# Cross keys halved into differences on PSUM scores, with part of the row maxima formed by ScalarE and VectorE together, in a post-norm decoder layer

## The chip, the cores and the metric

The kernel runs on one core of a Trainium2 chip. The metric is the device time of one execution in microseconds (us): the median of several runs. One core has TensorE (PE in the profile; its weight loads, PEld, overlap the matmuls), VectorE (DVE), ScalarE (ACT), GpSimd (POOL) and SyncE (SP), which issues most transfers.

## The reference, cut to what matters

```python
x = layernorm(x + linear_attention(x))                 # 16 heads of 64, relu features
q, k, v = heads(x @ Wq + bq), heads(x @ Wk + bk), heads(x @ Wv + bv)     # 8 x 512 tokens, 16 heads of 16
y  = softmax(causal(q @ k.T * scale)) @ v              # 512 keys
qc, kc, vc = heads(x @ Wcq + bcq), heads(ctx @ Wck + bck), heads(ctx @ Wcv + bcv)
y += softmax(qc @ kc.T * scale) @ vc                   # 1024 context keys: the cross attention
x = layernorm(x + y @ Wp + bp)
x = layernorm(x + top1_of_8_experts(x))                # 256 -> 1024 -> 256
```

Batch 8, 512 tokens, width 256, context 1024 x 128, all float32. The softmax subtracts the maximum of each query's scores over all of its keys.

## The kernel before, in words

A loop over the 8 batches does both attentions, and the experts follow once at the end. Inside a batch the second attention, the stretch that the change is about, works on 8 pairs of heads. The two heads of a pair (`a` = 0 and 1) lie on partitions 0 to 63 and 64 to 127 of `hq` and `hk`, so two neighbouring matmuls of different heads run on the two halves of TensorE's rows at the same time. Every head needs its scores twice.

- **Maxima units** (`("max", p, m)`, 22 a pair): scores with queries on the partitions, 128 queries by 512 keys, one matmul into one PSUM bank (`max_unit`), then one VectorE pass (`reduce`) writes the maximum of each row to `craw`. Sixteen of them are cross units (4 query tiles, 2 halves of the 1024 keys, 2 heads), read by a plain `reduce_max`; six are self units, read by `tensor_tensor_reduce` with the causal mask added.
- **Row units** (`("row", p, 0)`): the finished maxima `mpad` are turned by TensorE, and four ScalarE copies write them to `mrow`.
- **Exp units** (`("exp", p, n)`, 11 a pair: 3 own, 8 cross): scores with keys on the partitions, both heads, 4 matmuls of 512 columns in a cross unit. Two of them are the scores; the other two (`minus`, `mrow`) subtract the maximum inside PSUM (L826). Then one ScalarE exponential of 128 x 1024 goes to the ring `es`. The units use two slots of two banks in turn, so unit k waits for the exponential of k-2.
- **Weigh units**: the exponentials times the values, 8 matmuls into a bank of their own, `zbank`. After the last of a pair, `keep` (ScalarE, `zk`) copies it out, `turn` (TensorE L867) transposes it into a ring bank and ScalarE writes `zt`.

Maxima, rows and turns share three PSUM banks as a ring: each takes the bank that has been free longest, and TensorE waits for the last reader of that bank (`ring_slot`). In the first stretch of a batch there is a fourth bank, `zbank`.

`heads_order` writes one list, ORDER, which every engine follows in the same order. First come 30 maxima units (22 + `AHEAD` of 8), with projections between them (`FIRST_PARTS`). Then comes a loop in which each turn, called a **cycle** in this document, has on TensorE: one maxima unit (A), exp unit k, two maxima units (B, C), exp unit k+1, one maxima unit (D), two weigh units of four units earlier. 11 cycles make two pairs, called a **period** here. The maxima run ahead of the exponentials, so the last cycles of a batch have none.

`kc0` and `kc1` are the cross key projections: ScalarE writes their high part to `stage` and VectorE the rest (`high_part`, `low_part`).

## Time and profile before

| | us |
|---|---|
| median of 3 runs | 2242.48 (2242.23 to 2243.74) |
| the profiled execution | 2242.68 |
| its span in the profile | 2240.8 |
| one batch (start to start) | 235 |
| of it: 30 maxima units with projections between | 22 |
| of it: 44 cycles | 128 |

The profiled execution stands 0.20 us above the median, and 1.9 us of it lie outside the span, so a change of the span is read as a change of the time. One batch out of the middle of the loop (its second attention at 572 to 723 us) is read closely; the others are alike.

### The profile page before, as it was taken

Reading aid. Unit: us, or ns where it says so; the run is one execution under the profiler, and the core shown is the slowest. Engines: PE = TensorE matmul, PEld = TensorE weight load, DVE = VectorE, ACT = ScalarE, POOL = GpSimd, SP = SyncE. Lnnn points to the kernel's source line nnn. Section 1 sums busy time; section 2 is a strip of 40 time slices with the busy share of each in tenths; the row PEclk is TensorE's granted clock in tenths of the full one; section 3 lists DMA queues with packets and bytes.
Section 4 is the critical chain, followed back from the end, with each engine's and each line's share of the span. In section 5 each row is a group of like instructions: output and inputs, shape, how many; then the busy total and the mean of one; then the engine's idle time right before and its main releaser. Section 6 shows DMA issues by size and latency. Waiting matters only on the chain. (4 is left out here: it accounts for less than half of the span.)

```text
span 2240.8 us, 51067 instructions
## 1 busy us (share of the span) xinstructions
PE 2155.1 (96%) x16290; PEld 1349.3 (60%) x16291; DVE 1364.8 (61%) x3905; ACT 1100.7 (49%) x1680; POOL 367.4 (16%) x628
## 2 busy tenths in 40 slices
PE   8999999999999999999999999999999999799998
PEld 4555555556455555555555555565556455599997
DVE  2588358844784468645883588358844785354454
ACT  1267525761477237722774267525762477233332
POOL 1011111111111111111111111111111111122222
PEclk9999999999999999999999999999999999899999
DMA  7440035102610162005400450035102610755553
GB/s 239 158 167 25 1 110 204 47 2 86 226 49 2 65 224 72 2 11 208 141 2 11 153 173 25 1 108 204 48 2 86 226 49 1 245 186 179 177 182 110
DMA packets 115762, 235.74 MB, mean 105 GB/s; under 512 B 19614, under 2 KB 42655, under 8 KB 113344
## 3 DMA queue, kind: packets, MB, share of 16 engines
q1 hardware_dynamic: 112112, 224.23, 29.9%
q0 software_dynamic: 3408, 8.41, 1.0%
q8 instruction: 136, 2.23, 0.4%
q14 instruction: 106, 0.87, 0.1%
HBM read 154.04 MB, written 73.17 MB: 101 GB/s over the span
## 5 line engine op out<-in xcount | busy, mean ns | idle before, releaser
L1221 ACT ACTIVATE es<-ps 128x1024 f32<-128x1024 f32 (+1 forms) x704 | 665.0, 984 | 241.4 <-PE ps L826 178.7
L1432 DVE TENSOR_REDUCE craw<-ps 128x1 f32<-128x512 f32 x1024 | 636.0, 683 | 95.7 <-PE ps L790 93.9
L790 PE MATMUL ps<-hk,hq 64*128 64x512 f32 x1024 | 382.6, 449 | 13.3 <-DVE craw L1428 5.6
L824 PE MATMUL ps<-hq,hk 64*128 64x512 f32 x1024 | 323.1, 436 | 2.2 <-ACT es L1221 2.2
L826 PE MATMUL ps<-mrow,minus 64*128 64x512 f32 x1024 | 285.6, 390 | 0.0
L1428 DVE CUSTOM_DVE_ANT_0 ps<-ps,causal 128x512 f32<-128x512 f32 (+3 forms) x512 | 235.7, 519 | 74.7 <-PE ps L787 74.3
L790 PEld LDWEIGHTS ps<-hk,hq 64*128 64x128 f32 x1024 | 173.8, 184 | 177.3 <-DVE craw L1432 119.1
L856 PE MATMUL ps<-es,vca 128*17 128x256 f32 x4096 | 276.7, 382 | 1.1
L678 POOL TENSOR_SCALAR_AFFINE_SELECT es<-es 128x256 f32<-128x256 f32 x256 | 99.0, 406 | 619.6 <-ACT es L1221 619.4
L1751 ACT ACTIVATE hT<-ph,b1s 128x128 f32<-128x128 f32 x312 | 89.0, 368 | 183.3 <-PE ph L1714 183.3
L826 PEld LDWEIGHTS ps<-mrow,minus 64*128 64x128 f32 x1024 | 165.4, 185 | 10.6
L824 PEld LDWEIGHTS ps<-hq,hk 64*128 64x128 f32 x1024 | 141.9, 184 | 29.6 <-ACT es L1221 18.6
L856 PEld LDWEIGHTS ps<-es,vca 128*17 128x17 f32 x4096 | 93.8, 96 | 107.7 <-issue 35.7
L1714 PEld LDWEIGHTS ph<-xinT,w1s 128*128 128x128 f32 x1248 | 147.5, 194 | 3.0 <-issue 1.1
L1714 PE MATMUL ph<-xinT,w1s 128*128 128x128 f32 x1248 | 147.8, 277 | 0.7 <-ACT xinT L1741 0.7
L1727 PE MATMUL py<-w2s,hT 128*128 x624 | 141.1, 379 | 0.0
L787 PE MATMUL ps<-hk,hq 64*128 64x512 f32 (+3 forms) x512 | 139.0, 349 | 0.5
L876 PE MATMUL ps<-xT_s,wqf 128*128 128x512 f32 x288 | 138.4, 607 | 0.0
L886 PE MATMUL ps<-wkf,xT_s 128*128 128x512 f32 x288 | 130.3, 597 | 0.0
L817 PE MATMUL ps<-hq,hk 64*128 64x512 f32 (+3 forms) x512 | 125.6, 340 | 0.6
L1727 PEld LDWEIGHTS py<-w2s,hT 128*128 128x128 f32 x624 | 115.5, 190 | 14.1
L787 PEld LDWEIGHTS ps<-hk,hq 64*128 64x128 f32 x512 | 81.0, 184 | 66.1 <-issue 25.4
(210 smaller groups left out, 2833.4 us busy)
## 6 DMA issues: line engine op xcount, KB each, us to landing
w1s<-in_w1T SPq DMA_DIRECT2D x39, 1024.0 KB, 5.4
hk<-scr_kc SPq DMA_DIRECT2D x64, 512.0 KB, 5.1
scr_kc<-staged SPq DMA_DIRECT2D x16, 1024.0 KB, 4.2
scr_qc<-staged SPq DMA_DIRECT2D x32, 512.0 KB, 4.5
scr_q<-staged SPq DMA_DIRECT2D x32, 512.0 KB, 5.3
hq<-scr_qc SPq DMA_DIRECT2D x56, 256.0 KB, 4.5
hq<-scr_q SPq DMA_DIRECT2D x56, 256.0 KB, 4.2
hk<-scr_k SPq DMA_DIRECT2D x56, 256.0 KB, 4.6
```

What stands on the lines that cost most here:

```text
L787: last = mm(pb[:, col:col + w], hq[i][at, t * P:(t + 1) * P], hk[i][at, 0:w], start=True, stop=True)
L790: last = mm(pb, hq[i][at, T + t * P:T + (t + 1) * P], hk[i][at, T + half * BANK:T + (half + 1) * BANK], start=True, stop=True)
L824: mm(pb[a], hk[i][rows[a], T + j * P:T + (j + 1) * P], hq[i][rows[a], T:2 * T], start=True, stop=False)
L826: last = mm(pb[a], neg[a], mrow[p % 2][rows[a], :], start=False, stop=True)
L856: last = mm(z[row:row + VW, (2 - len(tiles)) * P:2 * P], (va if own else vca)[:, j, p * HB + a, :], weights, start=n in (0, NSELF), stop=n ...
L876: last = mm(t[:, a * T:(a + 1) * T], wqf[:, c, j * P:(j + 1) * P], xT_s[:, c, :], start=c == 0, stop=c == KC - 1)
L886: last = mm(t[:, half * 512:(half + 1) * 512], xT_s[:, c, i * P:(i + 1) * P], wkf[:, c, half * 512:(half + 1) * 512], start=c == 0, stop=c ...
L1221: nc.scalar.activation(es[:, k % ERING, :].rearrange("p (a c) -> p a c", a=HB)[:, :, 0:w], eslot[k % 2][:].rearrange("p (a c) -> p a c", a ...
L1428: last = v.tensor_tensor_reduce(own, own, causal[:, (NT - 1 - t) * P:NT * P], 1.0, LOWEST, ALU.add, ALU.max, craw[p % 2][:, t, a:a + 1, 0])
L1432: last = v.reduce_max(craw[p % 2][:, t, a:a + 1, 1 + half], pb, AX.X)
L1714: last = mm(ph[g % 2][:, a * TILE:(a + 1) * TILE], w1s[i][:, k, (GROUP * c + a) * P:(GROUP * c + a + 1) * P], xinT[i][:, k, :], start=k == ...
L1727: last = mm(py[i][:, n, 0:C], hT[i][:, c, n * P:(n + 1) * P], w2s[:, bass.ds(e * (NHC * C) + c * C, C)], start=c == 0, stop=c == NHC - 1)
```

## The change

The first half of the cross keys is stored as a difference: GpSimd subtracts the two halves of the context once a batch (`context_difference`), so that `kc` columns 0 to 511 hold key j minus key j+512, without bias, and columns 512 to 1023 hold the second half itself. Scores of the first half are then scores of the second half plus scores of the difference, and they are formed by adding a matmul onto the bank that still holds the former.

- Exp units: a cross tile of the second half is done as before. The tile of the first half ("rest") is two units later in the same slot and has two matmuls of differences only; the maximum is still subtracted there. Own and cross units are reordered so that each rest unit follows its tile by two.
- Maxima units: the rest unit of a query tile must use the same bank as its first unit. Therefore the ring is replaced by fixed places: head 0 always uses bank 1 (banks 1 and 3 in turn for the first pair), and head 1, rows and turns use banks 0 and 2 in turn.
- For head 1 and the last two query tiles the two halves are not added in PSUM. Unit "over" gets the differences and ScalarE writes their positive part to `over_s` (`maxima_over`); unit "upper" gets the second half, and VectorE adds `over_s` and takes the maximum in one pass. VectorE has 20 passes a pair in place of 22, ScalarE two more.
- `AHEAD` is 12 in place of 8 and `ROW_AFTER` (8, 6) in place of (4, 6); a cycle is now A, exp, B, exp, C, D, weigh, weigh.

```diff
-AHEAD = 8
-ROW_AFTER = (4, 6)
+AHEAD = 12
+ROW_AFTER = (8, 6)
...
+def cross_tile(c):
+    i = c // 4 * 2 + c % 2
+    return (i, True) if c % 4 >= 2 else (NTC // 2 + i, False)
+OWN_UNITS = [("own", i, False) for i in range(NSELF)]
+CROSS_UNITS = [("cross", *cross_tile(c)) for c in range(NTC)]
+UNITS = (OWN_UNITS + CROSS_UNITS, OWN_UNITS[:2] + CROSS_UNITS + OWN_UNITS[2:])
...
+BY_TILE = [("cross", t, rest) for t in range(NT) for rest in (False, True)]
+BY_TWO = [("cross", 2 * n + t, rest) for n in range(NT // 2) for rest in (False, True) for t in range(2)]
+SHARED = BY_TWO[:NT] + [("over" if over else "upper", t, False) for t in range(NT // 2, NT) for over in (True, False)]
+def max_of(p, m):
+    n, a = divmod(m, HB)
+    cross = SHARED if a else BY_TWO if p == 0 else BY_TILE
+    return (*(cross + SELF_MAX if p % 2 or p == 0 else SELF_MAX + cross)[n], a)
...
 def heads_order():
-        order += take(HB)
+        order += take(1)
         if k + 1 < steps:
             order.append(("exp", *divmod(k + 1, NU)))
-        order += take(1, True)
+        order += take(HB, True)
...
 def places():
-        at = min(banks, key=lambda i: last[i])
+        if kind == "max" and m % HB == 0:
+            at = (1, 3)[count[0] % 2] if p == 0 else 1
+            count[0] += 1
+        else:
+            at = (0, 2)[count[1] % 2]
+            count[1] += 1
...
 def exp_scores(b, p, n):
-                        mm(pb[a], hk[i][rows[a], T + j * P:T + (j + 1) * P], hq[i][rows[a], T:2 * T], start=True, stop=False)
-                    for a in turned:
-                        last = mm(pb[a], neg[a], mrow[p % 2][rows[a], :], start=False, stop=True)
+                        last = mm(pb[a], hk[i][rows[a], T + j * P:T + (j + 1) * P], hq[i][rows[a], T:2 * T],
+                                  start=not rest, stop=rest, skip_group_check=rest)
+                    if not rest:
+                        for a in turned:
+                            last = mm(pb[a], neg[a], mrow[p % 2][rows[a], :], start=False, stop=True)
...
+                def maxima_over(p, m):
+                    e, t = ("max", p, m), max_of(p, m)[1]
+                    act.wait_ge(s_ring, cur(b, NRING, RING_AT[e] + 1))
+                    if p:
+                        act.wait_ge(s_red, cur(b, NRED, RED_AT[UPPER[p - 1, t]]))
+                    nc.scalar.activation(over_s[:, t - NT // 2, :], mbank[PLACE[e]], ACT.Relu).then_inc(s_over, 1)
...
+                    elif what == "upper":
+                        dve.sem_inc(s_held, 1)
+                        dve.wait_ge(s_over, cur(b, NOVER, OVER_AT["max", p, m]))
+                        dve.sem_inc(s_held, 1)
+                        last = v.tensor_tensor_reduce(pb, pb, over_s[:, t - NT // 2, :], 1.0, LOWEST, ALU.add, ALU.max,
+                                                      craw[p % 2][:, t, a:a + 1, 1])
```

What this does to TensorE's order at the start of a batch is seen after the second half of projection `qf0` (the first row, L930 or L876, is the projection). A row is one matmul with the PSUM tensor written, its inputs and the semaphores that it waits for; ps0 holds banks 0 and 1, ps1 bank 2 and `zbank`, and `s_red` is raised when VectorE has read a bank. Before:

```order
L876 MATMUL ps3<-xT_s,wqf 128x512 x2
L767 REGISTER_ALU
L790 MATMUL ps0<-hk1,hq1 128x512 [waits s_red]
L767 REGISTER_ALU
L790 MATMUL ps0<-hk1,hq1 128x512 [waits s_red]
L767 REGISTER_ALU
L797 ISA [waits s_red]
L798 MATMUL ps1<-ident,mpad 128x128 [waits s_max]
L767 REGISTER_ALU
L790 MATMUL ps1<-hk1,hq1 128x512 [waits s_red]
L739 REGISTER_ALU
L876 MATMUL ps2<-xT_s,wqf 128x512 [waits s_act]
```

After:

```order
L930 MATMUL ps3<-xT_s,wqf 128x512 x2
L819 REGISTER_ALU
L842 MATMUL ps0<-hk1,hq1 128x512 [waits s_red]
L819 REGISTER_ALU
L842 MATMUL ps0<-hk1,hq1 128x512 [waits s_red]
L819 REGISTER_ALU
L842 MATMUL ps0<-hk1,hq1 128x512 [waits s_red]
L819 REGISTER_ALU
L842 MATMUL ps1<-hk1,hq1 128x512 [waits s_red]
L789 REGISTER_ALU
L930 MATMUL ps2<-xT_s,wqf 128x512 [waits s_act]
L930 MATMUL ps2<-xT_s,wqf 128x512
```

Before, three maxima units and the row unit stood here in four different banks. Now there are four units, and the first and the third (both of head 0) are in bank 1.

In the cycle in which an even pair's result is turned (here pair 2, units 3 and 4 of pair 3 exponentiated), TensorE's rows from exp unit k+1 on were, before (`es,va` are weigh units, `zk` the turn):

```order
L824 MATMUL ps2<-hq1,hk1 128x512 [waits s_exp]
L824 MATMUL ps2<-hq1,hk1 128x512
L826 MATMUL ps2<-mrow1,minus 128x512 x2
L767 REGISTER_ALU
L787 MATMUL ps0<-hk2,hq2 128x512 [waits s_red]
L840 REGISTER_ALU [waits s_keep]
L856 MATMUL ps1<-es,va 17x256 [waits s_cut]
L856 MATMUL ps1<-es,va 17x256 x3
L767 REGISTER_ALU
L867 MATMUL ps1<-ident,zk 128x128 [waits s_keep,s_red]
L867 MATMUL ps1<-ident,zk 128x128 x3
```

The same cycle after the change:

```order
L875 MATMUL ps2<-hq1,hk1 128x512 [waits s_exp]
L875 MATMUL ps2<-hq1,hk1 128x512
L819 REGISTER_ALU
L842 MATMUL ps0<-hk2,hq2 128x512 [waits s_red]
L819 REGISTER_ALU
L842 MATMUL ps0<-hk2,hq2 128x512 [waits s_red]
L894 REGISTER_ALU [waits s_keep]
L910 MATMUL ps1<-es,va 17x256 [waits s_cut]
L910 MATMUL ps1<-es,va 17x256 x3
L817 REGISTER_ALU
L921 MATMUL ps1<-ident,zk 128x128 [waits s_keep,s_over]
L921 MATMUL ps1<-ident,zk 128x128 x3
```

The two `mrow` matmuls are gone, and the turn no longer waits for a pass of VectorE but for `s_over`: its bank was last used by the over unit of this same cycle, which ScalarE reads.

ScalarE's rows around it, after the change (`s_ring` is raised by a maxima unit, `s_sc` by an exp unit):

```order
L1288 ACTIVATE es<-ps3 128x1024 [waits s_av,s_sc]
L1278 REGISTER_ALU
L1280 REGISTER_ALU [waits s_ring]
L1281 ACTIVATE r_s<-ps1 128x512 [waits s_red]
L1286 REGISTER_ALU
L1288 ACTIVATE es<-ps2 128x1024 [waits s_av,s_sc]
L1297 ACTIVATE zk<-ps1 128x512 [waits s_av]
L1286 REGISTER_ALU
L1288 ACTIVATE es<-ps3 128x1024 [waits s_av,s_sc]
L1278 REGISTER_ALU
L1280 REGISTER_ALU [waits s_ring]
L1281 ACTIVATE r_s<-ps1 128x512 [waits s_red]
```

The rows on `r_s` are the new positive parts (`over_s` lies in `r_s`). The second one is what the turn waits for, and ahead of it stand an exponential, `zk`, another exponential and the positive part of the cycle before.

## Rows read from the trace of the kernel before

**Rows 1.** The page: busy time of each engine, share of the span, instructions.

```profile
PE 2155.1 (96%) x16290; PEld 1349.3 (60%) x16291; DVE 1364.8 (61%) x3905; ACT 1100.7 (49%) x1680; POOL 367.4 (16%) x628
```

**Rows 2.** Busy time by stretch: first maxima, one period, last cycles of a batch.

```profile
core 0: us, PE busy (x) PEld busy (x) DVE busy (x) ACT busy (x) POOL busy (x), PEclk, DMA share, GB/s
565.00:594.50 29.50, 28.57 (x90) 13.10 (x89) 21.04 (x44) 8.94 (x15) 4.22 (x4) 1.00 0.77 264
657.00:690.20 33.20, 32.50 (x342) 19.38 (x338) 27.74 (x68) 24.54 (x36) 5.26 (x12) 1.00 0.01 2
702.10:722.80 20.70, 19.46 (x227) 9.53 (x223) 2.20 (x12) 17.11 (x23) 3.35 (x8) 1.00 0.01 2
```

**Rows 3.** Timeline of TensorE, one cycle: units A and D, weigh, next A.

```profile
626.61 0.49 PE L790 MATMUL ps<-hk,hq 64*128 64x512 f32 x1
...
627.93 0.46 PE L790 MATMUL ps<-hk,hq 64*128 64x512 f32 x1
...
628.32 1.06 PE L856 MATMUL ps<-es,vca 128*17 128x256 f32 x16
629.30 0.49 PE L790 MATMUL ps<-hk,hq 64*128 64x512 f32 x1
```

**Rows 4.** Timeline of VectorE over the same cycle.

```profile
627.14 2.48 DVE L1432 TENSOR_REDUCE craw<-ps 128x1 f32<-128x512 f32 x4 [0.21 <-PE ps L790]
```

**Rows 5.** Groups by line and shape: count, busy, mean ns, idle before.

```profile
L1432 DVE TENSOR_REDUCE craw<-ps 128x1 f32<-128x512 f32 x1024 | 636.0, 683 | 95.7 <-PE ps L790 93.9
L826 PE MATMUL ps<-mrow,minus 64*128 64x512 f32 x1024 | 285.6, 390 | 0.0
L790 PEld LDWEIGHTS ps<-hk,hq 64*128 64x128 f32 x1024 | 173.8, 184 | 177.3 <-DVE craw L1432 119.1 <-DVE craw L1428 27.3 <-ACT mrow L1213 12.7
L1428 DVE CUSTOM_DVE_ANT_0 ps<-ps,causal 128x512 f32<-128x512 f32 x128 | 86.0, 713 | 40.8 <-PE ps L787 40.8
```

**Rows 6.** Timeline of TensorE, first maxima of a batch up to cycle 1.

```profile
588.86 0.51 PE L790 MATMUL ps<-hk,hq 64*128 64x512 f32 x2
...
589.98 1.98 PE L876 MATMUL ps<-xT_s,wqf 128*128 128x512 f32 x4
...
592.56 1.98 PE L876 MATMUL ps<-xT_s,wqf 128*128 128x512 f32 x4
594.47 0.49 PE L790 MATMUL ps<-hk,hq 64*128 64x512 f32 x1
```

**Rows 7.** Timeline of TensorE, the cycle with a turn: 646.96 to 650.92.

```profile
644.70 0.49 PE L790 MATMUL ps<-hk,hq 64*128 64x512 f32 x1
...
646.96 0.49 PE L790 MATMUL ps<-hk,hq 64*128 64x512 f32 x1
...
649.34 0.66 PE L867 MATMUL ps<-ident,zk 128*128 128x128 f32 x4
649.92 1.06 PE L856 MATMUL ps<-es,va 128*17 128x128 f32 x20
650.92 0.44 PE L787 MATMUL ps<-hk,hq 64*128 64x384 f32 x1
```

**Rows 8.** Timeline of ScalarE in that cycle and the one before.

```profile
645.75 1.51 ACT L1221 ACTIVATE es<-ps 128x1024 f32<-128x1024 f32 x2 [0.91 <-PE ps L820]
647.15 0.61 ACT L1230 ACTIVATE zk<-ps 128x512 f32<-128x512 f32 x1
```

**Rows 9.** Timeline of TensorE, a cycle with a row unit.

```profile
655.78 0.32 PE L798 MATMUL ps<-ident,mpad 128*128 128x128 f32 x1 [0.18 <-DVE craw L1432]
656.04 1.06 PE L856 MATMUL ps<-es,vca 128*17 128x256 f32 x16
```

**Rows 10.** Timeline of both engines in a last cycle: two exp units, weigh, next.

```profile
717.86 0.50 PE L824 MATMUL ps<-hq,hk 64*128 64x512 f32 x2
...
717.98 1.94 ACT L1221 ACTIVATE es<-ps 128x1024 f32<-128x1024 f32 x2 [0.17 <-PE ps L826]
...
719.50 0.51 PE L824 MATMUL ps<-hq,hk 64*128 64x512 f32 x2
```

More of the change, by code:

```diff
@@ L133, in take @@
         taken = []
-        while maxima and (count or maxima[0][0] == "row") and (border or maxima[0] != ("row", PAIRS - 1, 0)):
+        while maxima and (count or border and maxima[0][0] == "row"):
             count -= maxima[0][0] == "max"
@@ L172, with is_over @@
 ORDER = heads_order()
+def is_over(entry):
+    return entry[0] == "max" and max_of(*entry[1:])[0] == "over"
 def reciprocals_later():
@@ L188 @@
 RING_AT = {e: n for n, e in enumerate(RING)}
-N_FIRST = sum(e[0] in ("max", "row") for e in ORDER[:ORDER.index(("exp", 0, 0))])
 def places():
-    place, former, last = {}, {}, [-1] * (MBANKS + 1)
-    for n, e in enumerate(RING):
-        banks = range(MBANKS + (n < N_FIRST))
-        at = min(banks, key=lambda i: last[i])
-        place[e], former[e], last[at] = at, RING[last[at]] if last[at] >= 0 else None, n
+    place, former, last, count = {}, {}, {}, [0, 0]
+    for e in RING:
+        kind, p, m = e
+        if kind == "max" and m % HB == 0:
[4 more added lines that the diff above has]
+            count[1] += 1
+        place[e], former[e], last[at] = at, last.get(at), e
+        if kind == "max" and max_of(p, m)[2]:
+            what, t, _, a = max_of(p, m)
+            assert former[e][0] == "max" and max_of(*former[e][1:]) == (what, t, False, a) and former[e][1] == p
     return place, former
 PLACE, SAME = places()
-NRING, NRED = len(RING), sum(e[0] == "max" for e in RING) + 1
+NRING, NOVER = len(RING), sum(is_over(e) for e in RING)
+NRED = sum(e[0] == "max" for e in RING) - NOVER + 1
 LAST_TURN = ("turn", PAIRS - 1, 0)
-RED_AT = {e: sum(f[0] == "max" or f == LAST_TURN for f in RING[:n + 1]) for n, e in enumerate(RING)}
+RED_AT = {e: sum(f[0] == "max" and not is_over(f) or f == LAST_TURN for f in RING[:n + 1]) for n, e in enumerate(RING)}
+OVER_AT = {e: sum(is_over(f) for f in RING[:n + 1]) for n, e in enumerate(RING)}
+UPPER = {(p, max_of(p, m)[1]): ("max", p, m) for p in range(PAIRS) for m in range(MAXES) if max_of(p, m)[0] == "upper"}
 NEXP = PAIRS * NU
-LAST_IN_Z = max(RED_AT[e] for e in RING if PLACE[e] == MBANKS)
+LAST_IN_Z = max(RED_AT[e] for e in RING if PLACE[e] == 3)
 TILE = 128
@@ L694, in _ @@
                 for kind, p, n in ORDER:
-                    if kind == "exp" and n < NSELF:
-                        cut(p, n)
+                    if kind == "exp" and UNITS[p % 2][n][0] == "own":
+                        cut(p, n, UNITS[p % 2][n][1])
                     elif kind == "turn" and p < PAIRS - 1:
@@ L770, in max_unit @@
             def max_unit(b, p, m):
-                n, a = divmod(m, HB)
+                what, t, rest, a = max_of(p, m)
                 i = p % SLOTS
-                if (n, a) == (0, 0):
+                if (what, t, rest, a) == ("cross", 0, False, 0):
                     if p == 0:
@@ L777, in max_unit @@
                     pe.wait_ge(s_cross[i], b * CROSS[i] + CROSS_AT[p])
-                if (n, a) == (2 * NT, 0):
+                if (what, t, a) == ("self", 0, 0):
                     if p == 0:
@@ L783, in max_unit @@
                 pb, at = ring_slot(b, ("max", p, m)), slice(a * HROW, (a + 1) * HROW)
-                if n >= 2 * NT:
-                    for t, col in MAX_SELF[n - 2 * NT]:
-                        w = (t + 1) * P
-                        last = mm(pb[:, col:col + w], hq[i][at, t * P:(t + 1) * P], hk[i][at, 0:w], start=True, stop=True)
-                else:
-                    t, half = divmod(n, 2)
-                    last = mm(pb, hq[i][at, T + t * P:T + (t + 1) * P],
-                              hk[i][at, T + half * BANK:T + (half + 1) * BANK], start=True, stop=True)
+                if what == "self":
+                    for u, col in MAX_SELF[t]:
+                        w = (u + 1) * P
+                        last = mm(pb[:, col:col + w], hq[i][at, u * P:(u + 1) * P], hk[i][at, 0:w], start=True, stop=True)
+                else:
+                    keys = hk[i][at, T:T + BANK] if rest or what == "over" else hk[i][at, T + BANK:T + TC_]
+                    last = mm(pb, hq[i][at, T + t * P:T + (t + 1) * P], keys, start=not rest, stop=True, skip_group_check=rest)
                 last.then_inc(s_ring, 1)
@@ L809, in exp_scores @@
                 rows = [slice(a * HROW, (a + 1) * HROW) for a in range(HB)]
-                w = int(n >= NSELF)
+                what, j, rest = UNITS[p % 2][n]
+                w = int(what == "cross")
                 neg = [minus[at, w:w + 1].broadcast_to([HROW, P]) for at in rows]
-                turned = range(HB - 1, -1, -1)
-                if n < NSELF:
-                    for j, col in EXP_SELF[n]:
+                turned = (0, 1) if k % 2 else (1, 0)
+                if what == "own":
+                    for j, col in EXP_SELF[j]:
                         w = T - j * P
@@ L843, in weigh @@
                 z = zbank[:, 0:T // 2] if own else zbank[:, T // 2:T]
[L844 removed]
+                for j, col in (EXP_SELF[i] if own else [(i, 0)]):
                     first = j if own else 0
@@ L1288, in _ @@
             v.memset(blank, 0.0)
+            for n in range(2):
+                v.memset(craw[n][:], LOWEST)
             v.memset(mpad[:], 0.0)
@@ L1462, in _ @@
                 for kind, p, n in DVE_ORDER:
-                    if kind == "max":
+                    if kind == "max" and not is_over((kind, p, n)):
                         reduce(p, n)
```

70 lines of the change are left out of this document (46 added, 24 removed).

## Prediction

> **What bounds the kernel now.** I read the page first: TensorE is busy for 96% of the span, VectorE for 61%, ScalarE for 49% [rows 1]. By that alone TensorE is the bound and every matmul taken away is time won. Then I read the stretches of one batch, since the share is a mean. In one period of the maxima and exponentials (33.2 us) TensorE has 32.5 us busy, VectorE 27.7, ScalarE 24.5, but TensorE's weight loads only 19.4 [rows 2]. A matmul here has a mean of 390 ns [rows 5], although two of them on different row halves start every 0.23 us or so; its busy time holds pipeline depth and waiting. So I went to the timeline.
>
> In a regular cycle unit A starts at 626.61, D at 627.93, the weigh units at 628.32 and the next A at 629.30 [rows 3]. That is 1.32 + 0.39 + 0.98 = 2.69 us. VectorE starts on A at 627.14, 0.53 us after the matmul, and does four passes in 2.48 us, 0.62 each; before them it sat idle 0.21 us waiting for TensorE [rows 4]. A pass has a mean of 683 ns [rows 5], so A's pass ends at 627.82, and D, the fourth unit on a ring of three banks and thus in A's bank, starts 0.11 us later. The 1.32 us are therefore a round trip: matmul, 0.53 us, pass, release of the bank (0.79 us after the pass began). The work between A and D fits inside it. The 119.1 us that weight loads of L790 wait for VectorE [rows 5] are such places. A cycle is a latency chain A, pass, D, weigh, A, and neither engine's sum.
>
> The reader is to see that taking matmuls out of the stretch from A to D saves nothing as long as the round trip stays.
>
> **The Trainium skill on this reading.** "Trainium Kernel Development and Optimization", section Performance Expectations, says that matmul busy time is a bad measure of how near TensorE is to its limit, and that weight load time is a better one. By the former the removed matmuls would be worth their columns (the first rival below), by the latter TensorE has room. This trace agrees with the page: 32.5 of 33.2 us against 19.4 [rows 2].
>
> **The change, part by part.**
>
> *Matmuls removed.* Half of the 1024 `mrow` matmuls of the cross units [rows 5] go: 512, side by side in pairs, 256 slots of about 0.23 us, 59 us in all. In regular cycles they lie between A and D, under the round trip: 0.
>
> *Fixed places.* Head 0 is always in bank 1. The cycle is now A, exp, B, exp, C, D, and C must wait for A's bank. That is the same round trip, 1.32 us, now ahead of C. D (head 1) comes behind it with a weight load of its own; a load takes 184 ns [rows 5] and overlaps the former in part, so I take 0.1, bounds 0 and 0.18. A regular cycle: 1.32 + 0.1 + 0.39 + 0.98 = 2.79 us, against 2.69. The four cycles of a period without a keep, turn or self unit pay this, as do others.
>
> *VectorE passes.* Two per pair less (1.24 us). VectorE already waits in each cycle [rows 4], so 0 on the chain. The new pass with a second operand is not in the trace; the nearest is the masked one, 713 ns for 512 columns against 683 [rows 5]. With a float32 operand from SBUF I take the same; even 0.3 us more would fall into VectorE's 5.5 us of idle time per period [rows 2]. 0, bound +0.3 per pair.
>
> *ScalarE's positive part.* 128 x 512, not in the trace: nearest are the narrower exponential (1.51 less 0.92, thus 0.59 us) and `zk` (0.61) [rows 8]; starts follow each other after about 0.5 us. ScalarE has 8.7 us idle per period [rows 2] and two pairs cost 2.0, so mostly hidden. What is queued behind it is the next exponential and everything after. This hurts in one place, the turn of an even pair, whose bank was just used by an over unit. Before: the turn at 649.34, 4.64 us after the start (644.70) of the cycle before it; then 0.58 us to the weigh units and 1.00 to the next cycle [rows 7]. Now, from the same start: first exponential at 1.05 [rows 7, 8], positive part at 1.97, exponential at 2.46 (now 1024 wide in place of the narrow one), `zk` at 3.38, exponential at 3.87, positive part 4.79 to 5.38, the turn at about 5.45. The two cycles take 7.03 us, not 6.22: +0.8. Without this wait it would be +0.1 to +0.2. Behind the waiting turn stand all weigh units and the next maxima, so nothing covers it.
>
> *The other special cycles*, worked out the same way (release 0.79 after the start of a pass, self passes by the 713 ns row). A row unit waits for the second pass, 0.53 + 0.62 + 0.79 = 1.94, then 0.26 and 0.99: 3.19 us as now [rows 9]. The self units of an odd and an even pair now follow each other in bank 1, and cost about +0.2 in the odd turn's cycle (a round trip begun later, as VectorE still holds an upper unit), -0.2, +0.5 and -0.4 in the next three; a keep cycle with the narrow own unit gains 0.25. The sum over the eleven cycles is 33.8 us against 33.2 now [rows 2], and 33.1 in the period before it: +0.7, bounds -0.5 (no 0.1 for D and no wait at the turn) and +1.6 (0.18 for D, 0.3 per new pass).
>
> *The first maxima of a batch.* Here bank 1's round trip has no exp units above it. Before: 588.86 to 594.47, 5.61 us, with two projection halves of 1.91 [rows 6] between. After, from the same point: a group with two head-0 units, 1.32 + 0.1 + 0.33; a half, 1.91; a group in which moreover an over unit waits for the second pass, 1.94 + 0.31; a half, 1.92; and, as `AHEAD` is 12, a third group with the round trip of 1.32 before cycle 1. Together 9.15: +3.5 us. Bounds +2 (banks freed by 0.3 earlier in each of three groups, and VectorE, with two passes less to do, brings 0.5 into it) and +4. The earlier groups use four banks as before and stay.
>
> *The last cycles.* The maxima end one cycle earlier. That cycle was 3.4 us and becomes 2.1: -1.3. In the seven others each rest unit is 0.23 us shorter, but ScalarE's two exponentials take 1.94 us, the second exp unit waits for one (717.86), and its own chain to the next cycle is 1.64 [rows 10]. ScalarE is busy 17.1 of 20.7 us there [rows 2]. I take 0.1 a cycle, -0.6 (bounds 0 and -1.6). Sum -1.9, bounds -1.3 and -2.9.
>
> *Keys and context.* GpSimd is busy 16% of the span [rows 1] and subtracts for the next batch at the end of this one: 0. `kc1` is two ScalarE instructions and not one, ahead of VectorE's copy of `x1T`: +0.1 a batch, bounds 0 and 0.2.
>
> **Sum for a batch.** First maxima +3.5; cycles 1 to 3, 0; cycles 4 to 10, which are a period's last seven, +0.8; two periods +1.4; last cycles -1.9; keys +0.1. Together +3.9, times 8 is +31 us. Against the profiled execution of 2242.7, which is 0.2 above the median, this gives 2274 us. With the bounds, taken not all at one end, +1.2 to +6.5 a batch: 2252 to 2295.
>
> **Rivals.** *TensorE's columns count.* If D waits less than I think and cycles shrink with what they hold, 59 us go, and the first maxima still cost 3.5 x 8 = 28: 2242.7 - 59 + 28 = 2212; with those hidden too 2184, with half the gain 2241. For it: 32.5 of 33.2 us busy [rows 2]. Against it: A to D equals the round trip to 0.11 us [rows 3, 4]. It decides if C or D starts under 1.2 us after A. *VectorE's relief counts.* 27.7 us of 33.2 is the highest share after TensorE's [rows 2]; with 1.24 us less a pair a period would be up to 2.5 shorter, 2242.7 - 8 x 3 x 2.5 + 28 = 2211. Against it: its 0.21 us of idle time in every cycle. The two together: chance 0.18. "Perfetto Trace Analysis", section Optimizing Scalar/DVE Operations, advises giving work of a saturated DVE to ScalarE; by it the second rival would hold. The trace does not bear it out here, as VectorE waits in every cycle. *The banks cost less:* the turn does not wait and D comes at once; then +1.5 a batch, 2255, slower still: 0.12. *No change,* the first maxima costing 2 and the cycles gaining 0.3 each period: 2242 to 2246, 0.08.
>
> **Chances.** My forecast 0.62, the others as above. A measurement of this kernel tells about 0.2% (4.5 us) from no change. Faster 0.19, same 0.07, slower 0.74. The range that leaves out no more than 2 in 10 reaches from 2230 (part of the first rivals) to 2294; the likeliest case's own range is 2252 to 2295.
>
> **What would show it.** In the profile after: regular cycles of about 2.8 us with C 1.3 us after A and TensorE idle before it; the even turn at about 5.4 us from the start of the cycle before, released by ScalarE's `r_s`; the stretch from 588.86's counterpart to the first exp unit 9 us; weight loads of maxima units waiting for VectorE clearly above today's 119 us; busy VectorE about 80 us lower without a shorter span. Wrong would be cycles of 2.5 us or less, or a turn that is not held.

## The result and the profile after

| | before | after |
|---|---|---|
| median (us) | 2243.11 (2242.23 to 2243.82) | 2302.38 (2301.38 to 2304.52) |
| ratio | | 1.0265, 95% interval 1.025 to 1.0279 |
| profiled span | 2240.8 | 2299.7 |

The kernel is 59 us slower. The direction was forecast, the size (+31) was half of it, and the time lies above the range. First the page after, for [rows 1]:

```profile
PE 2139.2 (93%) x15778; PEld 1288.1 (56%) x15779; DVE 1334.8 (58%) x3907; ACT 1155.4 (50%) x1824; POOL 381.4 (17%) x637
```

TensorE and VectorE have less to do in a longer span. The groups after, with the columns of [rows 5]:

```profile
L1512 DVE TENSOR_REDUCE craw<-ps 128x1 f32<-128x512 f32 x768 | 501.5, 685 | 196.6 <-PE ps L842 192.4
...
L842 PEld LDWEIGHTS ps<-hk,hq 64*128 64x128 f32 x1024 | 143.7, 184 | 243.7 <-DVE craw L1512 196.4 <-issue 35.3 <-DVE craw L1503 10.3
...
L879 PE MATMUL ps<-mrow,minus 64*128 64x512 f32 x512 | 121.6, 392 | 0.0
...
L1509 DVE CUSTOM_DVE_ANT_0 ps<-ps,r_s 128x512 f32<-128x512 f32 x128 | 89.5, 699 | 23.2 <-ACT r_s L1281 23.2
```

Weight loads of maxima units wait 196 us for VectorE (119 before) while VectorE waits 192 us for those matmuls (94 before): each waits for the other. The new pass (L1509) has a mean of 699 ns, near the masked one's 713 [rows 5]. VectorE's busy time fell by 30 us and not by the 80 that the prediction names as a sign: 256 plain passes are gone (636.0 to 501.5 us), but 128 new ones came (89.5 us). The windows after: one period and the last cycles, for [rows 2]:

```profile
core 0: us, PE busy (x) PEld busy (x) DVE busy (x) ACT busy (x) POOL busy (x), PEclk, DMA share, GB/s
...
676.95:711.47 34.52, 32.11 (x327) 17.34 (x324) 26.95 (x69) 26.16 (x38) 5.36 (x13) 1.00 0.01 2
725.20:746.10 20.90, 19.48 (x224) 8.83 (x225) 0.95 (x5) 18.19 (x25) 3.75 (x8) 1.00 0.01 2
```

The period grew from 33.2 to 34.52 us at a full clock, with less busy time on TensorE. TensorE's timeline at the end of the first maxima, for [rows 6] (605.32 answers to 588.86, 614.52 to 594.47):

```profile
602.90 0.57 PE L842 MATMUL ps<-hk,hq 64*128 64x512 f32 x2 [1.09 <-DVE craw L1503]
603.40 1.98 PE L930 MATMUL ps<-xT_s,wqf 128*128 128x512 f32 x4
605.32 0.50 PE L842 MATMUL ps<-hk,hq 64*128 64x512 f32 x2
606.60 0.57 PE L842 MATMUL ps<-hk,hq 64*128 64x512 f32 x2 [0.78 <-DVE craw L1512]
607.10 1.98 PE L930 MATMUL ps<-xT_s,wqf 128*128 128x512 f32 x4
...
610.30 1.09 PE L842 MATMUL ps<-hk,hq 64*128 64x512 f32 x2 [0.52 <-DVE craw L1512]
...
614.52 0.49 PE L842 MATMUL ps<-hk,hq 64*128 64x512 f32 x1 [0.78 <-DVE craw L1512]
```

In every group the third unit, of head 0, waits for the pass on the first. The first row is one group earlier; its third unit waits 1.09 us for a self pass. TensorE's timeline of the cycle before the even turn and of the turn's, for [rows 7]:

```profile
666.94 0.50 PE L842 MATMUL ps<-hk,hq 64*128 64x512 f32 x1
...
668.32 0.48 PE L842 MATMUL ps<-hk,hq 64*128 64x512 f32 x2
668.73 0.63 PE L910 MATMUL ps<-es,vca 128*17 128x256 f32 x8
669.50 0.49 PE L842 MATMUL ps<-hk,hq 64*128 64x512 f32 x1
...
672.38 0.66 PE L921 MATMUL ps<-ident,zk 128*128 128x128 f32 x4 [0.19 <-ACT r_s L1281]
...
674.17 0.50 PE L842 MATMUL ps<-hk,hq 64*128 64x512 f32 x1
```

and VectorE's and ScalarE's beside it:

```profile
668.76 0.69 DVE L1512 TENSOR_REDUCE craw<-ps 128x1 f32<-128x512 f32 x1 [0.58 <-PE ps L842]
...
670.78 1.05 ACT L1288 ACTIVATE es<-ps 128x1024 f32<-128x1024 f32 x1
671.69 0.64 ACT L1281 ACTIVATE r_s<-ps 128x512 f32<-128x512 f32 x1
```

A starts at 666.94 and C, in the same bank, at 668.32: that is the round trip I had counted. But C's pass starts at 668.76 and the next A, again in bank 1, at 669.50: a second round trip in the same cycle, 1.18 us, which I had not. The turn starts 5.44 us after 666.94 (forecast 5.45), released by the positive part that stands behind exponentials. Since ScalarE holds the turn, the second round trip cost nothing in these two cycles; where nothing else holds TensorE, it does (see the cycles below). The two cycles take 7.23 us, not 7.03: behind the turn 1.20 us pass to the next A (672.97 to 674.17), 1.00 before [rows 7]. Here the Trainium skill ("Perfetto Trace Analysis", Optimizing Tensor Performance) bears: independent matmul groups should rotate through different PSUM banks, so that emptying one overlaps the next. The trace agrees: units that come back to a bank after two places wait, 0.78 us in the rows above.

Stretches of one batch, in us, read from the timelines of each kernel (start to start; zk is the copy of a pair's result, 0 to 7):

| kernel | first maxima to first exp | to zk 1 | zk 3 to 5, a period | zk 5 to 7 |
|---|---|---|---|---|
| before | 22.46 | 34.97 | 33.21 | 27.13 |
| after | 26.60 | 36.91 | 34.52 | 25.41 |
| e8_places | 26.70 | 35.31 | 33.60 | 26.38 |
| e2_over_first | 26.58 | 36.35 | 33.93 | 25.18 |
| e1_pad | 26.62 | 36.89 | 34.52 | 26.44 |
| e5_two_banks | 25.01 | 36.87 | 34.54 | 25.39 |
| e6_exp_only | 23.63 | 36.29 | 34.60 | 26.88 |
| e15_ring_fit | 26.31 | 36.30 | 34.01 | 26.57 |
| e17_ring_mixed | 22.36 | 35.83 | 33.63 | 26.79 |
| e19_ring_mixed_pad | 22.40 | 36.02 | 34.07 | 27.88 |

The period by its cycles, in us from A to A in the same batch. The eleven cycles are lettered as in the expectations below, and these letters are not those of the units: cycle C holds the odd turn and cycle I the even one, and in before cycles F and K hold row units. The cycle of [rows 3] is a B; 666.94 is the start of an H.

| cycle | before | e8_places | e2_over_first | after | e17_ring_mixed |
|---|---|---|---|---|---|
| C, odd turn | 3.67 | 3.94 | 3.94 | 4.04 | 3.95 |
| D | 2.71 | 2.64 | 2.86 | 2.86 | 2.49 |
| E | 3.02 | 3.19 | 3.70 | 3.70 | 2.69 |
| F | 3.19 | 2.70 | 2.70 | 2.69 | 3.10 |
| H | 2.26 | 2.78 | 2.56 | 2.57 | 2.49 |
| I, even turn | 3.98 | 4.15 | 4.13 | 4.66 | 4.28 |
| A, B, G, J, K | 14.35 | 14.22 | 14.00 | 14.00 | 14.61 |
| sum | 33.18 | 33.62 | 33.89 | 34.52 | 33.61 |

### The profile page after: what moved, and what is told of

Its sections match the earlier page's. It is cut to its first block and busy times, and to the rows that moved or that the text cites. A ratio compares the mean times of both kernels' runs of the same rounds, so it can differ in the third digit from the quotient of the medians.

```text
span 2299.7 us, 50687 instructions
## 1 busy us (share of the span) xinstructions
PE 2139.2 (93%) x15778; PEld 1288.1 (56%) x15779; DVE 1334.8 (58%) x3907; ACT 1155.4 (50%) x1824; POOL 381.4 (17%) x637
## 5 line engine op out<-in xcount | busy, mean ns | idle before, releaser
L1512 DVE TENSOR_REDUCE craw<-ps 128x1 f32<-128x512 f32 x768 | 501.5, 685 | 196.6 <-PE ps L842 192.4
L842 PE MATMUL ps<-hk,hq 64*128 64x512 f32 x1024 | 332.6, 467 | 52.1 <-DVE craw L1512 25.2
L910 PE MATMUL ps<-es,vca 128*17 128x256 f32 x4096 | 295.4, 383 | 0.0
L842 PEld LDWEIGHTS ps<-hk,hq 64*128 64x128 f32 x1024 | 143.7, 184 | 243.7 <-DVE craw L1512 196.4
L875 PE MATMUL ps<-hq,hk 64*128 64x512 f32 x1024 | 270.8, 444 | 7.5 <-ACT es L1288 4.4
L875 PEld LDWEIGHTS ps<-hq,hk 64*128 64x128 f32 x1024 | 124.8, 185 | 62.6 <-ACT es L1288 52.6
L839 PE MATMUL ps<-hk,hq 64*128 64x512 f32 (+3 forms) x512 | 119.2, 362 | 21.4 <-DVE craw L1503 15.4
L930 PE MATMUL ps<-xT_s,wqf 128*128 128x512 f32 x288 | 138.4, 607 | 0.0
L879 PE MATMUL ps<-mrow,minus 64*128 64x512 f32 x512 | 121.6, 392 | 0.0
L964 PE MATMUL ps<-big_b,x_s 128*128 128x512 f32 x256 | 119.9, 606 | 1.8 <-ACT big_b L1201 1.1
L839 PEld LDWEIGHTS ps<-hk,hq 64*128 64x128 f32 x512 | 67.5, 184 | 89.9 <-DVE craw L1503 71.2
L1061 PE MATMUL ps<-big_c,big_a 128*128 128x256 f32 x512 | 112.6, 381 | 2.9 <-ACT big_c L1241 2.9
```

Of the source, the lines that this page charges most:

```text
L839: last = mm(pb[:, col:col + w], hq[i][at, u * P:(u + 1) * P], hk[i][at, 0:w], start=True, stop=True)
L842: last = mm(pb, hq[i][at, T + t * P:T + (t + 1) * P], keys, start=not rest, stop=True, skip_group_check=rest)
L875: last = mm(pb[a], hk[i][rows[a], T + j * P:T + (j + 1) * P], hq[i][rows[a], T:2 * T], start=not rest, stop=rest, skip_group_check=rest)
L879: last = mm(pb[a], neg[a], mrow[p % 2][rows[a], :], start=False, stop=True)
L910: last = mm(z[row:row + VW, (2 - len(tiles)) * P:2 * P], (va if own else vca)[:, j, p * HB + a, :], weights, start=n == 0, stop=True, skip ...
L930: last = mm(t[:, a * T:(a + 1) * T], wqf[:, c, j * P:(j + 1) * P], xT_s[:, c, :], start=c == 0, stop=c == KC - 1)
```

## Experiments

Before ran beside every group of kernels, with medians of 2243.15 to 2243.62 us.

**e8_places: order and places alone.** The kernel before, with the order in a cycle, `AHEAD`, `ROW_AFTER` and `places()` of after; none of the new arithmetic, and own and self units where they were before.

```diff
-        order += take(HB)
+        order += take(1)
...
-        at = min(banks, key=lambda i: last[i])
+        if kind == "max" and m % HB == 0:
+            at = (1, 3)[count[0] % 2] if p == 0 else 1
```

> The kernel before (every unit with all its matmuls, no positive part on ScalarE, all 22 passes on VectorE), with only the order and the places of the kernel after: 34 maxima units ahead, A, exp, B, exp, C, D, head 0 always in bank 1. Theory (bank 1's two round trips in a cycle, C behind A and the next A behind C, cost the time): nearly all of the loss is here, 2280 to 2305 us, with a period of 34 us or more. Rival (the new work does it: the positive part on ScalarE, the pass with a second operand, the waits for ScalarE at the turns): 2243 to 2260 us.

Measured 2280.2 (ratio 1.0164, 1.0147 to 1.0181): +37 us. So most of the loss, not nearly all of it, is the schedule, and its period is 33.6 us, not the 34 or more that I expected. The table says where: +4.2 of its +4.6 us a batch are the first maxima, and a period has only +0.4. The order in a cycle and the places changed together here; no run parts them.

**e2_over_first: positive parts earlier.** On after:

```diff
+        if is_over(e) and order[n - 1][0] == "exp":
+            order[n - 1], order[n] = e, order[n - 1]
```

> The kernel after, ScalarE taking each positive part ahead of the exponential that it stood behind. Theory (the turn of the even pairs waits for the positive part behind two exponentials): the turn starts some 0.8 us earlier, three or four times a batch, 2277 to 2290 us. Rival (the wait at the turn is covered, or the exponential that is now later costs as much): 2297 to 2307 us.

Measured 2286.77: 15.6 us less than after. TensorE's timeline, cycle start and turn:

```profile
662.20 0.50 PE L854 MATMUL ps<-hk,hq 64*128 64x512 f32 x1
...
667.10 0.66 PE L933 MATMUL ps<-ident,zk 128*128 128x128 f32 x4
```

The turn now comes 4.90 us after that start, without a wait. The mechanism holds, 0.54 us at an even turn and 0.10 at an odd one (cycle C above).

**e1_pad: the removed columns put back.** On after, in a rest unit:

```diff
+                    if rest:
+                        for a in turned:
+                            last = mm(pb[a], nought[rows[a], 0:1].broadcast_to([HROW, P]), mrow[p % 2][rows[a], :], ...
```

> The kernel after, with two matmuls of zero weights added to each rest unit of the exponentials, so that all removed columns are back. Theory (a cycle is a chain of round trips): they fall into TensorE's waiting, +0 to +12 us on the kernel after (2302 to 2314), most of it in the last cycles of a batch. Rival (the columns count): 256 slots of 0.23 us, +59 us, 2361.

Measured 2307.8: +5.4 us. The page's groups show that both sorts of matmul are there, at one price:

```profile
L880 PE MATMUL ps<-mrow,nought 64*128 64x512 f32 x512 | 122.5, 391 | 0.0
L884 PE MATMUL ps<-mrow,minus 64*128 64x512 f32 x512 | 121.2, 390 | 0.0
```

The new group is 122.5 us of matmuls, TensorE's busy time rises by 34.5 us (2139.2 to 2173.7, as the matmuls overlap others), and the period stays at 34.52 us. Only zk 5 to 7 grows. The columns did not count, and this rival falls for the kernel as it is. The median hides a little of their price: undisturbed batches start 243.49 us apart, not 242.46, which is 8.2 us in all, but after lost some 2 us in two batches to what e1_pad's trace does not show (1.2 of it to the granted clock, see the last section).

**e5_two_banks: more banks for the first maxima.** On after:

```diff
-            at = (1, 3)[count[0] % 2] if p == 0 else 1
+            at = (1, 3)[count[0] % 2] if p == 0 or p == 1 and m < 8 else 1
```

So that the places fit, these units also take the query tiles in the order of pair 0.

> The kernel after, in which the first eight maxima units of pair 1 (still ahead of the exponentials) have banks 1 and 3 in turn for head 0 and not bank 1 alone. Theory (each unit that waits for its neighbour but one in bank 1 costs 0.5 to 0.8 us there, as nothing else lies between): 1.5 to 2.5 us less a batch, 2282 to 2291 us. Rival (the projections that stand between set the pace of that stretch): 2298 to 2306 us.

Measured 2290.56: 11.8 us less, 1.59 us a batch in the first column of the table and nothing elsewhere. Of the groups above, the one with 1.09 us of waiting has 0.27 left and the one with 0.78 none; the last two keep 0.38 and 0.78.

**e22_over_and_banks: both.**

> e2_over_first and e5_two_banks together on the kernel after. Theory (two separate waits at different places of a batch): their gains of 15.6 and 11.8 us add up, 2273 to 2278 us. Rival (they overlap): 2279 to 2288 us.

Measured 2273.52 (1.0135, 1.012 to 1.0151): 28.9 us less than after, where the two gave 27.4. They are separate terms.

**e6_exp_only: differences on the old ring.** The kernel before, rest units with two matmuls, and for half of the maxima units two matmuls added in a bank, followed by the same pass:

```diff
+                    last = mm(pb, hq[i][at, T + t * P:T + (t + 1) * P], hk[i][at, T + BANK:T + TC_], start=True, stop=half == 1)
+                    if half == 0:
+                        last = mm(pb, hq[i][at, T + t * P:T + (t + 1) * P], hk[i][at, T:T + BANK], start=False, stop=True)
```

> The kernel before with its ring of three banks and its order; keys as differences, rest units of the exponentials with two matmuls in place of four; the maxima of the lower half of the keys by two matmuls added in PSUM, with the same passes on VectorE. Theory (matmuls removed in the cycles bring nothing, only the last cycles of a batch gain, and the extra maxima matmuls lie under the round trip at a small cost): 2233 to 2250 us. Rival (the columns count): 512 matmuls come out in 256 slots of 0.23 us, and 512 go in, in part beside others: up to -59 and +0 to +59 us, and the period's length moves with what it holds, by over 0.5 us.

Measured 2284.96: +42 us, far outside what I expected, and the period is 34.60. TensorE's and VectorE's timelines of cycle B (L806 and L809 are the first and the added matmul):

```profile
674.34 0.50 PE L806 MATMUL ps<-hk,hq 64*128 64x512 f32 x1
674.68 0.39 PE L809 MATMUL ps<-hk,hq 64*128 64x512 f32 x1
...
675.90 0.45 PE L806 MATMUL ps<-hk,hq 64*128 64x512 f32 x1
677.27 0.49 PE L806 MATMUL ps<-hk,hq 64*128 64x512 f32 x1
```

```profile
675.11 2.49 DVE L1460 TENSOR_REDUCE craw<-ps 128x1 f32<-128x512 f32 x4 [0.44 <-PE ps L809]
```

VectorE starts 0.77 us after A and not 0.53 [rows 3, 4], D 1.56 us after it, and the cycle takes 2.93 us, not 2.69. I had put the added matmul under the round trip, but it stands in it. Six of the eleven cycles grow by 0.23 or 0.24 us like this one and cycle A by 0.17; cycles D, F and J do not change and cycle I loses 0.15. So here a removed matmul beside the chain gives nothing in most cycles, and an added one ahead of the pass costs all of its 0.24 us where the chain runs through it.

**e9_d_later.** The kernel before, D moved behind the weigh units:

```diff
-        order += take(1)
+        order += take(2 if k else 1)
...
-        order += take(1, True)
```

> The kernel before, with unit D of each cycle moved behind the two weigh units, next to A of the following cycle. Theory (a cycle of before is held by the round trip from A to D in one bank; the work between is shorter by some 0.1 us, and VectorE idles 0.21 us a cycle): cycles of 2.5 to 2.6 us in place of 2.69, 2205 to 2235 us. Rival (TensorE's own work fills the cycle, the round trip is covered): 2239 to 2247 us.

Measured 2365.79 (1.0551): +122 us, my worst miss but one. TensorE's and VectorE's timelines:

```profile
698.11 0.50 PE L789 MATMUL ps<-hk,hq 64*128 64x512 f32 x2
...
698.91 0.97 PE L789 MATMUL ps<-hk,hq 64*128 64x512 f32 x2
699.47 0.59 PE L816 MATMUL ps<-hq,hk 64*128 64x384 f32 x2
...
700.33 1.06 PE L855 MATMUL ps<-es,vca 128*17 128x256 f32 x16
701.32 0.50 PE L789 MATMUL ps<-hk,hq 64*128 64x512 f32 x2
```

```profile
694.77 2.68 DVE L1431 TENSOR_REDUCE craw<-ps 128x1 f32<-128x512 f32 x4 [0.35 <-PE ps L789]
698.64 2.48 DVE L1431 TENSOR_REDUCE craw<-ps 128x1 f32<-128x512 f32 x4 [1.19 <-PE ps L789]
```

D and A start at 698.11, B at 698.91, and C, which needs D's bank, just ahead of 699.47. The round trip has moved to D and the next C, and there only one exp unit lies beside it: the other (699.47 to 700.33) and the weigh units follow behind, and the cycle takes 3.21 us. VectorE idles 1.19 us in it, not 0.21. In the kernel before both exp units lie beside the round trip.

**e12_ring: all new arithmetic on three banks.** After's units are listed so that first and rest unit stand three places apart:

```diff
+    for t in range(NT // 2):
+        for rest in (False, True):
+            rows += [("cross", t, rest, a) for a in range(HB)]
+            rows.append(("upper" if rest else "over", t + NT // 2, False, 1))
...
+            banks = [i for i in range(3 + (late < N_FIRST)) if i not in held.values()]
+            at = min(banks, key=lambda i: last[i])
```

> All of the new arithmetic of the kernel after (two matmuls in rest units, differences added in PSUM, positive parts on ScalarE), but on the ring of three banks of the kernel before with its 30 maxima ahead and its order in a cycle: maxima units are listed so that a tile's first and rest unit stand three places apart and so share a bank without any fixed place. Theory (the fixed bank of head 0 costs the time, the arithmetic little): 2235 to 2258 us. Rival (the arithmetic costs it: the positive part and its waits): 2275 us or more.

Measured 2298.55 (1.0247). By this my theory seemed to fall. The trace showed waits of this kernel's own. TensorE's longest, by line (L881 is the row, L953 the turn; the last numbers are us in total, how often, and the longest):

```profile
PE ps L881 <- ACT r_s L1313: 20.8, 24, 0.9
PE ps L953 <- DVE craw L1535: 18.4, 24, 0.8
PE ps L881 <- DVE mpad L1551: 11.5, 8, 1.4
```

Rows wait for a positive part in their bank and turns for a self pass, about 39 us in all; before has neither wait (its rows wait 8.6 us for plain passes). The third, of the last row, is 6.7 us in before; here that row stands too early. TensorE's timeline there and the windows around it (the last number but two of a window is the granted clock) are

```profile
726.10 0.46 PE L881 MATMUL ps<-ident,mpad 128*128 128x128 f32 x1 [1.44 <-DVE mpad L1551]
```

```profile
690.00:723.00 33.00, 30.73 (x302) 17.59 (x302) 23.78 (x58) 24.32 (x37) 4.24 (x10) 1.00 0.01 2
723.00:727.00 4.00, 2.56 (x25) 1.49 (x25) 2.92 (x16) 2.77 (x5) 1.07 (x2) 0.89 0.00 0
727.00:730.00 3.00, 3.00 (x24) 0.98 (x22) 0.00 (x0) 1.75 (x4) 0.00 (x0) 0.57 0.00 0
```

**e13_ring_later, e14_ring_later_over.** e12 with D behind the weigh units, and that with positive parts earlier.

> As e12_ring, and unit D moved behind the weigh units as in e9_d_later, so that no round trip lies inside a cycle. Theory (removed matmuls pay where no round trip covers them, VectorE's 0.62 us a pass is the next bound, 2.3 to 2.5 us a cycle): 2170 to 2215 us, below both kernels. Rival (the matmuls removed pay nowhere in the cycles): within 10 us of e9_d_later.

> As e13_ring_later, with each positive part taken ahead of the exponential that it stood behind. Theory (the bank and VectorE's second pass wait for ScalarE): 3 to 15 us under e13_ring_later. Rival (nothing waits for it on this ring): within 3 us.

Measured 2381.74 and 2384.97. I had expected 2170 to 2215, and this is the farthest miss; it is 16 us above e9_d_later. e9's loss is there again (a period of 38.1 us, 37.6 in e9), and moving the positive parts ahead gains nothing.

**e10_self_last.** e2 with the self units last in every pair:

```diff
-ROW_AFTER = (8, 6)
+ROW_AFTER = (8, 10)
...
-    return (*(cross + SELF_MAX if p % 2 or p == 0 else SELF_MAX + cross)[n], a)
+    return (*(cross + SELF_MAX)[n], a)
```

> As e2_over_first, with the self units last in every pair (in the kernel after they come first in even pairs), rows set so that the places still fit. Theory (self units, whose passes come in two parts, lengthen bank 1's round trips in cycles D and E, 3.70 us where e8_places has 3.19): 0.5 to 0.8 us less a period, 2272 to 2281 us. Rival (their cost only moves to other cycles): 2284 to 2292 us.

Measured 2296.73, 10 us more than e2. Cycles D and E fell from 2.86 and 3.70 to 2.65 and 2.78 us, but four others grew, F from 2.70 to 3.19 as it now holds the row: the period is 34.33. The cost moved, as the rival says, and grew, beyond its 2292.

**e15_ring_fit, e16_ring_fit_over.** As e12, with the last row where it was; in odd pairs four self units stand first, so that rows and turns fall between groups:

```diff
+LISTS = (groups() + APART, APART + groups(), first_order())
```

> As e12_ring, with the list of an odd pair shifted by four units, so that every unit, row and turn stands exactly three places behind the last user of its bank, as in the kernel before, no row or turn follows a positive part in its bank, and the last row stands behind exp unit k+1 again. All of the new arithmetic is in it. Theory (distance 2 in the places costs the time): 2225 to 2256 us. Rival (the arithmetic costs it): 2270 us or more.

> As e15_ring_fit, with each positive part ahead of the exponential that it stood behind. Theory (a bank or VectorE's upper pass waits for it): 2 to 10 us less than e15_ring_fit. Rival (the ring leaves room for it): within 2 us.

Measured 2286.0 and 2283.0, which can't be told apart (ranges 2281 to 2290 and 2277 to 2297). By their expectations this speaks for the rival once more, but the trace again shows a wait of the list's own. Pair 1's self keys were asked for too soon: TensorE waits for their transfer, 3.00 us in this batch and 1.20 to 3.84 in the others. TensorE's timeline, and two windows, with the clock:

```profile
602.13 0.60 PE L877 MATMUL ps<-hk,hq 64*128 64x512 f32 x2 [3.00 <-DMA hk<-scr_k]
602.65 2.97 PE L968 MATMUL ps<-xT_s,wqf 128*128 128x512 f32 x4
```

```profile
585.00:598.00 13.00, 12.60 (x45) 6.37 (x46) 10.22 (x19) 5.79 (x9) 2.54 (x2) 1.00 0.80 265
...
602.60:605.60 3.00, 3.00 (x8) 0.87 (x6) 1.41 (x4) 0.00 (x0) 0.00 (x0) 0.65 1.06 411
```

**e17_ring_mixed: both waits taken out.** Pair 1 has its self units last; the others of the odd pairs begin with an over, a self, the upper and a self unit.

```diff
+    rows = [("over", NT // 2, False, 1), ("self", 0, False, 0), ("upper", NT // 2, False, 1), ("self", 0, False, 1)]
```

> As e15_ring_fit (all new arithmetic on a ring with distance 3 everywhere), without the two waits that its trace shows and that belong to its list and not to the ring: pair 1 has its self units last again (e15 waited 3.00 us for the transfer of their keys, and the clock fell behind it, 4 us a batch), and odd pairs begin with an over unit, a self unit, the upper unit and a self unit in place of four self units (e15's cycle K took 3.97 us, 3.19 before). Theory (the places cost the time, the arithmetic nothing or less): 4 us and three times 0.8 us less a batch, 2225 to 2245 us, at or under the kernel before. Rival (the arithmetic costs it): 2260 us or more.

Measured 2254.82 (1.0049, 1.0035 to 1.0063). It is +11 us on before and 48 us under after, with all of after's arithmetic. It lies above my theory's 2245 and below the rival's 2260, so neither is right in full. The window of one period:

```profile
649.58:683.19 33.61, 32.59 (x327) 18.44 (x323) 25.97 (x68) 26.19 (x39) 5.34 (x12) 1.00 0.10 35
```

**e19_ring_mixed_pad: e17 with the columns put back.**

> As e17_ring_mixed, with two matmuls of zero weights in each rest unit of the exponentials, so that all columns are back. Theory (chain of round trips on this ring too): 3 to 12 us more than e17_ring_mixed, mostly in the last cycles. Rival (on a ring without the short distances the removed matmuls pay in full): 30 to 59 us more.

Measured 2270.83: +16 us, between theory and rival. On this ring the removed matmuls pay more than in after, by the medians three times (16 us for 5.4), by the distance of undisturbed batches twice (2.2 us a batch for 1.0). They pay in some cycles too: 34.07 us a period against 33.63, where cycle D takes 2.72 and not 2.49 us and cycle I 4.50 and not 4.27.

**e20_mixed_own_first, e21_mixed_own_over.** e17 with the three own units first in odd pairs, and that with earlier positive parts:

```diff
-UNITS = (OWN_UNITS + CROSS_UNITS, OWN_UNITS[:2] + CROSS_UNITS + OWN_UNITS[2:])
+UNITS = (OWN_UNITS + CROSS_UNITS,) * 2
```

> As e17_ring_mixed, with the three own units first in odd pairs too, as in the kernel before. Theory (the wide own unit at the end of odd pairs makes the weigh units behind the even turn 0.2 us longer and cycle H 0.24 us): 0.4 to 0.7 us less a period, 2243 to 2250 us, about the kernel before. Rival (its cost moves to other cycles): 2252 to 2258 us.

> As e20_mixed_own_first, each positive part ahead of the exponential that it stood behind. Theory (with distance 3 nothing waits for it): within 4 us of e20_mixed_own_first. Rival: over 5 us less, as in e2_over_first.

Measured 2260.87 and 2263.15. Own units first are 6 us worse than e17, above both expectations, so the new order of own units is no cost on the whole, and the positive parts again make no difference on this ring (ranges 2258.7 to 2264.0 and 2261.7 to 2264.1).

## Why the prediction was half right

The prediction's own terms, for a batch:

| term | predicted | measured |
|---|---|---|
| first maxima | +3.5 | +3.96 |
| cycles 1 to 3 | 0 | +0.67 |
| cycles 4 to 10 | +0.8 | +0.98 |
| two periods | +1.4 | +2.76 |
| last cycles | -1.9 | -1.34 |
| keys | +0.1 | 0.0 |
| outside the eight batches' common length | 0 | +0.34 |
| sum | +3.9 | +7.4 |

Undisturbed batches start 242.46 us apart after and 235.46 before. These 7.0 us are the rows above the keys, so the keys cost nothing that shows; the +0.34 (2.7 us in all) came once in the profile: a fallen clock, a longer wait in one batch and a later start.

- **What bounds the kernel** was right: a latency chain and no engine's sum. e1_pad shows it on after. e9_d_later shows the same from the other side: what counts is how much work lies beside the round trip, and the kernel before has both exp units there.
- **"In regular cycles they lie between A and D, under the round trip: 0"** was right for the matmuls removed (+5.4 us if put back, most of it at the end of a batch), in after's places. On a ring of distance 3 they are worth 16 us.
- **"A regular cycle: 2.79 us"** was right for most (2.69 to 2.78); cycle B takes 2.56.
- **The even turn** was placed rightly (5.44), but "Without this wait it would be +0.1 to +0.2" for its two cycles was not: e2_over_first has 6.70 us there against 6.22, +0.5. The wait is worth 0.54. Of the rest, 0.20 are the weigh units behind the turn, where the reordering puts the wide own unit: with own units first (e20_mixed_own_first) they take 0.99 us again, not 1.20, though the turn there comes 0.24 us later.
- **The step that failed is the sum over the eleven cycles, "33.8 us against 33.2"**: 34.52. Its mechanism, a chain of round trips, was right; the cycles around the turns and self units were mis-sized, and a period grew by 1.34 us where I had +0.7. The largest error is cycle D, the first behind the odd turn (+0.15 for -0.2). I followed bank 1 from A to C and then let the weigh units hide the way back from C to the next A. Where VectorE comes late to C, they don't. TensorE's and VectorE's timelines:

```profile
656.02 0.58 PE L839 MATMUL ps<-hk,hq 64*128 64x512 f32 x2
...
657.77 0.44 PE L839 MATMUL ps<-hk,hq 64*128 64x384 f32 x1 [0.39 <-DVE craw L1503]
```

```profile
656.96 0.70 DVE L1503 CUSTOM_DVE_ANT_0 ps<-ps,causal 128x512 f32<-128x512 f32 x1
```

Unit C starts at 656.02, its pass 0.94 us later, behind a self pass and two small operations, and the next A waits until 657.77. The other errors are elsewhere: in cycles C (+0.37 for +0.2) and E (+0.68 for +0.5) the way from unit A to unit C is longer than the 1.32 us that I took (1.59 and 1.62), as VectorE holds an upper unit or A's self pass comes in two parts; the turn's two cycles have +0.99 for +0.8, the 0.20 of the weigh units above. By the cycle table, the order and places give 0.4 of the 1.34 and the positive parts behind exponentials 0.6; the last 0.3 are what cycles D and E cost with self units first (0.7), less what cycle H and others give back. In e10_self_last the self units' part moved to other cycles, so it is not a price of a unit that can be taken alone.
- **Cycles 1 to 3, "0"** failed by the same step: cycle 1 has no weigh units, so its way back from C is bare. C starts at 615.84 and the next A at 617.07, after 0.62 us of waiting for VectorE.
- **First maxima:** the stretch that I worked out took 9.20 us for 9.15. The groups ahead of it, which I had said would "stay", grew by 0.37 us. e5_two_banks shows that the waits it took away, 1.59 us, are bank 1's.
- **Last cycles:** mis-sized by 0.6 us. The cycles with rest units did shorten, but the one of the last even turn grew from 3.29 to 3.83 us. With own units first in every pair (before, e8_places, e20_mixed_own_first) it takes 3.29, with after's order of them (e2_over_first, e17_ring_mixed) 3.83: it is the reordering of own units, to which I gave no price.
- **The rivals.** TensorE's columns count: no in after, in part on the ring of e17. VectorE's relief counts: no, as VectorE's idle time grew instead. Banks cost less: no.

In all, of 59 us the order in a cycle and the places make 37. The arithmetic of after, with its reordering of self and own units, adds 22 in those places, of which 16 are positive parts that stand behind exponentials; with distance 3 for every bank it adds 11, and there it costs nothing that positive parts stand behind exponentials. What these 11 us are made of is open: e19_ring_mixed_pad says that the rest of the arithmetic costs 27 and the removed matmuls give back 16, but no run here parts the positive parts, the upper passes and the reordering. No version here beats the kernel before.

## What to carry to other kernels

Before a matmul is taken out, find the chain that sets the cycle: work beside it is worth little, work inside it its full time. When accumulation ties a unit to a bank, count how many places lie between two uses of each bank (three everywhere before, two for half of the units after) and follow the bank all the way round the loop, not only to its next user. A change that frees an engine but shortens that distance is better tried first as a reordering alone.

## What the runs showed of the hardware

- One matmul added onto a bank ahead of its pass moved the pass by 0.24 us (0.77 for 0.53) and the cycle by as much.
- The granted clock stood at 0.57 of full speed in the 3 us behind a wait of 1.44 us (e12_ring), and at 0.65 behind one of 3.00 us (e15_ring_fit): in part the lower level of 1.2 GHz. There the wait cost more than its length; the projection behind the second took 2.97 us where others take 1.98. But not each such wait did it. e12_ring has the wait of 1.44 us in all eight batches; the clock fell in three of them, whose last stretch takes 29.5 us and not 28.0.
- Short waits are no guarantee. The period after, which is full of waits of 0.8 us and less, ran at 1.00. But once in the same trace, in the first batch, it fell to 0.50 from the end of a cycle E (209 us) on, behind that cycle's waits of 0.38, 0.30 and 0.38 us, and the period took 35.75 us, not 34.52. TensorE's timeline and the window:

```profile
207.58 0.46 PE L839 MATMUL ps<-hk,hq 64*128 64x256 f32 x2 [0.30 <-DVE craw L1503]
208.42 0.32 PE L849 MATMUL ps<-ident,mpad 128*128 128x128 f32 x1 [0.38 <-DVE craw L1503]
```

```profile
209.00:212.00 3.00, 3.00 (x24) 1.50 (x18) 0.75 (x2) 0.94 (x5) 0.00 (x0) 0.50 0.03 8
```

The same waits stand in every cycle E of that trace. Why the clock fell at this one, no run here shows.
